# A perceiver block on one core: fp4 weight units loaded and dequantised in another rhythm, with zero products in the last context tiles

## The chip, the cores and the metric

One core of one Trainium2 chip runs the whole program. The metric is the device time in microseconds of one execution, as the median of several runs. The program drives five instruction streams: TensorE (PE) for matrix products and transposes, VectorE (DVE), ScalarE (ACT), GpSimd (POOL) and SyncE (SP), which here only issues DMA transfers. [...]

## What is computed

A latent array x of 64 rows and 256 columns passes three residual layers.

```python
x = x + cross_attention(layernorm(x), ctx)       # ctx: 6272 x 256, 32 heads of 8, q and k RMS-normalised
x = x + self_attention(layernorm(x))             # 16 heads of 128; wq, wk, wv, wo are fp4 codes times scales
x = x + expert_ffn(layernorm(x))                 # shared expert of 352, top 2 of 8 experts of 176
# the weights of the second layer:
w = codes * repeat(scales, 32, axis=0)           # one scale for 32 rows of a column
```

The codes and scales arrive as fp32. The product `codes * scales` has to be done on the chip for all four matrices, 256 x 2048 each for q, k and v, and 2048 x 256 for o.

## The kernel before

The cross attention streams the context in T = 49 tiles of 128 rows. For a tile, SP loads it transposed (`load`), DVE rounds it to `ctx_hi` (L544), POOL makes the rest `ctx_lo` (L348), and PE projects it to keys and values in six products of 512 columns (L796, L799, L802). ACT squares the keys (L419), DVE sums (L550), ACT makes the inverse root (L429, L433), DVE scales the keys (L568) and casts them to two fp16 parts (L575), POOL makes the third part (L354), and SP transposes the parts into `kT` by a DMA transpose (`turn`, L276). Then PE makes the scores with the 64 queries (L764, 32 products of 64 columns), ACT their exponentials in two halves (L407), and PE the weighted values, which gather in one PSUM bank over all tiles (L775).

The stages run against each other, staggered. In step c, PE does the scores of tile c, the values of tile c-1 and the projection of tile c+5; DVE and ACT normalise the keys of tile c+4, POOL makes `ctx_lo` of tile c+6 and the third key part of tile c+3. The scores of a tile wait until both exponentials of the tile before are done. PE, ACT and DVE run steps 2 to 41 in a hardware loop of eight steps a pass; steps before and behind are written out. POOL and SP are written out entirely. From step 44 there is no tile left to project.

The second layer's weights are cut into UNITS = 16 units of 128 x 1024 numbers: 12 of q, k and v (their scales are 128 x 512, used for both halves) and 4 of o (scales 128 x 1024). `w_all` keeps all of them; the scales pass through a ring of two buffers, `s_ring`. SP issues in step t of its own list `turn(t-7)` and `load(t)`, then at every third t the codes of a unit (one DMA of 512 KB, L279) and one t later its scales (L285, 256 KB read, or L288, 512 KB). POOL does `w = w * s` for a whole unit in one instruction (L340) behind the key part of every third step from step 3. Five small transfers (biases, the gate and its ids) go out at t = 2 to 6 (L313). Behind all of these SP issues the expert weights, five rounds of 704 KB and 352 KB (L293, L294).

Behind the loop DVE copies the gathered values (`o_sb`, L597), PE transposes them (L811), does 16 products of zeros (`keep_busy`, L725) while DVE makes x1 and its layer norm, transposes h (L718), waits for all units, and projects (L824). The output projection is L875, the experts L914 and L930.

```python
u, piece = divmod(t - LAG, DEQ)                  # SP: LAG = 7, DEQ = 3
if 0 <= u < UNITS and piece == 0: load_codes(u)
if 0 <= u < UNITS and piece == 1: load_scales(u)
```

Of the kernel before, what the change touches and what calls it, by code (L numbers as in the profile page):

```python
# [19 lines left out]
ALU = mybir.AluOpType  # L20
AX_X = mybir.AxisListType.X

P = 128
N = 64
D = 256
DC = D // P
# [19 lines left out]
RING = 2  # L46
# [3 lines left out]
UNITS = 4 * NSL  # L50
E, TOPK, H, HS = 8, 2, 176, 352
# [10 lines left out]
DEQ0, DEQ = 3, 3  # L62
# [51 lines left out]
def perceiver(nc, x, ctx_t, xwq, xwkv, codes, scales, wo_scales, qkv_bias, bo, gate_w, gate_bias,  # L114
              up_w, down_w, eye, expert_ids, out):
    with ExitStack() as stack:
# [26 lines left out]
        s_ring = sb("s_ring", [P, RING, WS])  # L143
# [90 lines left out]

        codes_in = [sem(f"codes_in{k}") for k in range(RING)]
        scales_in = [sem(f"scales_in{k}") for k in range(RING)]
        ring_free = [sem(f"ring_free{k}") for k in range(RING)]

# [20 lines left out]
        def _(sp):  # L259
# [18 lines left out]
            def load_codes(u):  # L278
                sp.dma_start(w_all[:, u], codes[:, u]).then_inc(codes_in[u % RING], 16)  # L279

            def load_scales(u):

                sp.wait_ge(ring_free[u % RING], u // RING + 1)
                if u < NQKV:
                    sp.dma_start(s_ring[:, u % RING, 0:512], scales[u].unsqueeze(0).to_broadcast(  # L285
                        [P // NB, NB, 512])).then_inc(scales_in[u % RING], 16)
                else:
                    sp.dma_start(s_ring[:, u % RING], wo_scales[u - NQKV].unsqueeze(0).to_broadcast(  # L288
                        [QB, P // QB, WS])).then_inc(scales_in[u % RING], 16)
# [11 lines left out]
            for t in range(2, T + LAG):  # L301
# [4 lines left out]
                u, piece = divmod(t - LAG, DEQ)  # L306
                if 0 <= u < UNITS and piece == 0:
                    load_codes(u)
                if 0 <= u < UNITS and piece == 1:
                    load_scales(u)  # L310
                if 2 <= t < 2 + len(small):
                    dst, src = small[t - 2]
                    sp.dma_start(dst, src).then_inc(ready("small_in"), 16)  # L313
# [7 lines left out]
        def _(pool):  # L321
# [4 lines left out]
            for k in range(RING):  # L326
                pool.memset(s_ring[0:1, k, 0:1], 0.0).then_inc(ring_free[k], 1)
# [3 lines left out]
            def dequantise(u):  # L331

                pool.wait_ge(codes_in[u % RING], (u // RING + 1) * 16)
                pool.wait_ge(scales_in[u % RING], (u // RING + 1) * 16)
                if u < NQKV:
                    w = w_all[:, u].rearrange("p (c n) -> p c n", c=DC)
# [5 lines left out]
            for c in range(FIRST, LAST + 1):  # L342
# [16 lines left out]
                if 0 <= u < UNITS and piece == 0:  # L359
                    dequantise(u)  # L360
# [653 lines left out]
```

## Time and profile before

| what | us |
|---|---|
| median of 3 runs | 228.83 |
| lowest and highest | 228.49 and 233.12 |
| the profiled execution | 229.14 |
| its span, first to last instruction | 227.3 |

In the span PE is busy 201.3 us, DVE 132.6, ACT 148.0 and POOL 107.4. The profile's times within the span count from its start. Matrix products are pipelined, so their recorded durations overlap; the distance of two starts says what one costs. An fp32 product is recorded as two. "PEclk" is the clock that PE was granted, as a share of 2.4 GHz (0.50 is 1.2 GHz); in a stretch with a change it is a mean. The words "<-issue" behind an idle time say that the engine waited for nothing that the profile shows.

### The profile page before, as it was taken

Reading aid. Unit: us, or ns where it says so; the run is one execution under the profiler, and the core shown is the slowest. Engines: PE = TensorE matmul, PEld = TensorE weight load, DVE = VectorE, ACT = ScalarE, POOL = GpSimd, SP = SyncE. Lnnn points to the kernel's source line nnn. Section 1 sums busy time; section 2 is a strip of 40 time slices with the busy share of each in tenths; the row PEclk is TensorE's granted clock in tenths of the full one; section 3 lists DMA queues with packets and bytes.
Section 4 is the critical chain, followed back from the end, with each engine's and each line's share of the span. In section 5 each row is a group of like instructions: output and inputs, shape, how many; then the busy total and the mean of one; then the engine's idle time right before and its main releaser. Section 6 shows DMA issues by size and latency. Waiting matters only on the chain.

```text
span 227.3 us, 9309 instructions
## 1 busy us (share of the span) xinstructions
PE 201.3 (89%) x3757; PEld 131.7 (58%) x3757; DVE 132.6 (58%) x324; ACT 148.0 (65%) x285; POOL 107.4 (47%) x125
## 2 busy tenths in 40 slices
PE   7786699799999999999999999898673899998994
PEld 2454477477777767676777777575452433554442
DVE  1668648367776776886867868757200422644721
ACT  3355688598989889889898898879852012413230
POOL 4334547746677586775785876847620000000000
PEclk9799999999999999999999999999758599999999
DMA  5418999999899799999998989899989860000000
GB/s 187 126 29 199 191 262 214 205 170 214 219 229 213 216 203 221 219 186 252 234 207 208 269 185 250 199 269 181 240 242 338 213 164 9 3 0 0 0 3 12
DMA packets 66674, 39.66 MB, mean 174 GB/s; under 512 B 53863, under 2 KB 60455, under 8 KB 66655
## 3 DMA queue, kind: packets, MB, share of 16 engines
q1 hardware_dynamic: 66223, 38.95, 78.2%
q10 hardware_dynamic: 432, 0.46, 0.6%
q8 instruction: 12, 0.20, 0.4%
q14 instruction: 7, 0.06, 0.1%
HBM read 26.48 MB, written 0.07 MB: 117 GB/s over the span
## 4 chain that ended last, share of the span: by engine, by line
PE 57%; issue 14%; ACT 9%; DVE 8%; DMA 7%; POOL 2%; SPq 1%; ACTq 0%; DVEq 0%
PE ps L775 12%; PE ps L796 8%; PE ps L764 6%; PE ps L802 6%; PE ps L799 6%; DMA kT<-k 5%; PE ps L824 5%; ACT room L407 4%; PE ps L914 3%; PE ps L930 2%; PE ps L725 2%; ACT k_sq L419 2%; ACT k_ln L429 2%; PE ps L875 2%; DVE k_n L568 2%
## 5 line engine op out<-in xcount | busy, mean ns | idle before, releaser
L407 ACT ACTIVATE room<-ps 128x1024 f32<-128x1024 f32 x98 | 100.2, 1027 | 15.8 <-PE ps L764 15.4
L348 POOL TENSOR_TENSOR ctx_lo<-ctx_f,ctx_hi 128x256 fp32r<-128x256 f32 x49 | 36.4, 743 | 53.3 <-DVE ctx_hi L544 51.2
L775 PE MATMUL ps<-room,v_flat 128*17 128x128 f32 x1568 | 55.9, 284 | 3.5 <-issue 3.5
L796 PE MATMUL ps<-wkv_hi,ctx_hi 128*128 128x512 f32 x98 | 43.4, 443 | 3.2 <-DVE k_n L568 1.7
L775 PEld LDWEIGHTS ps<-room,v_flat 128*17 128x17 f32 x1568 | 40.4, 100 | 7.5 <-issue 4.0
L575 DVE CAST k<-k_n 128x512 f16<-128x512 f32 x49 | 40.5, 826 | 2.6
L799 PE MATMUL ps<-wkv_lo,ctx_hi 128*128 128x512 f32 x98 | 39.0, 398 | 0.4 <-DVE wkv_lo L500 0.4
L340 POOL TENSOR_TENSOR w_all<-w_all,s_ring 128x1024 f32<-128x1024 f32 x16 | 38.0, 2380 | 0.0
L568 DVE TENSOR_TENSOR k_n<-ps,k_r 128x256 f32<-128x256 f32 x49 | 20.8, 425 | 25.5 <-ACT k_r L433 25.5
L354 POOL TENSOR_TENSOR k<-k_n,k 128x256 f16<-128x256 f32 x49 | 33.1, 675 | 3.5 <-DVE k L575 3.5
L764 PEld LDWEIGHTS ps<-qT,kT 24*128 24x128 f16 x1568 | 15.1, 94 | 28.0 <-ACT room L407 14.3
L802 PE MATMUL ps<-wkv_hi,ctx_lo 128*128 128x512 f32 x98 | 31.2, 400 | 0.0
L550 DVE TENSOR_REDUCE k_ss<-k_sq 128x32 f32<-128x256 f32 x49 | 20.4, 415 | 16.6 <-ACT k_sq L419 15.9
L764 PE MATMUL ps<-qT,kT 24*128 24x64 f16 x1568 | 21.2, 192 | 9.4 <-ACT room L407 3.5
L796 PEld LDWEIGHTS ps<-wkv_hi,ctx_hi 128*128 128x128 f32 x98 | 18.3, 187 | 16.1 <-issue 10.7
L429 ACT ACTIVATE k_ln<-k_ss,eps_rms 128x32 f32<-128x32 f32 x49 | 16.0, 327 | 9.5 <-DVE k_ss L550 9.5
L802 PEld LDWEIGHTS ps<-wkv_hi,ctx_lo 128*128 128x128 f32 x98 | 18.7, 191 | 4.4
L419 ACT ACTIVATE k_sq<-ps 128x256 f32<-128x256 f32 x49 | 18.5, 378 | 3.7 <-PE ps L802 3.7
L799 PEld LDWEIGHTS ps<-wkv_lo,ctx_hi 128*128 128x128 f32 x98 | 18.6, 190 | 2.9 <-DVE wkv_lo L500 0.8
L559 DVE COPY v_flat<-ps 128x256 f32<-128x256 f32 x45 | 18.6, 412 | 0.0
L544 DVE CAST ctx_hi<-ctx_f 128x256 fp32r<-128x256 f32 x48 | 13.6, 283 | 0.1
L365 ACT ACTIVATE rs<-mv,eps_ln 64x1 f32<-64x1 f32 x3 | 0.9, 294 | 19.3 <-DVE mv L475 19.3
(113 smaller groups left out, 137.0 us busy)
## 6 DMA issues: line engine op xcount, KB each, us to landing
w_all<-codes SPq DMA_DIRECT2D x16, 512.0 KB, 4.5
ctx_f<-ctx_t SPq DMA_DIRECT2D x48, 128.0 KB, 3.2
up_sb<-up_w SPq DMA_DIRECT2D x5, 704.0 KB, 9.7
s_ring<-scales SPq DMA_DIRECT2D x12, 256.0 KB, 3.8
s_ring<-wo_scales SPq DMA_DIRECT2D x4, 512.0 KB, 5.0
dn_sb<-down_w SPq DMA_DIRECT2D x5, 352.0 KB
kT<-k SPq DMA_TRANSPOSE x49, 4.0
wkv_f<-xwkv ACTq DMA_DIRECT2D x1, 256.0 KB, 3.1
```

Of the source, the lines that this page charges most:

```text
L340: nc.gpsimd.tensor_tensor(w, w, s, ALU.mult).then_inc(ring_free[u % RING], 1)
L348: nc.gpsimd.tensor_tensor(ctx_lo[:, split.slot(2)], ctx_f[:, split.slot(4)], ctx_hi[:, split.slot(2)].bitcast(F32), ALU.subtract).then_inc ...
L354: nc.gpsimd.tensor_tensor(key_part(keys, 2), k_n[:, keys.slot(2)].rearrange("p (h d) -> p h d", d=XD), key_part(keys, 0), ALU.subtract).th ...
L407: nc.scalar.activation(probs[:, t.slot(2), banks].rearrange("p g n -> p (g n)"), ps[:, banks, :].rearrange("p g n -> p (g n)"), ACT.Exp).t ...
L419: nc.scalar.activation(k_sq[:, a], ps_kv[a][:, 0:D], ACT.Square).then_inc(sq_done, 1)
L568: nc.vector.tensor_tensor(kn, ps_kv[r.slot(2)][:, 0:D].rearrange("p (h d) -> p h d", d=XD), k_r[:, r.slot(2)].unsqueeze(2).to_broadcast([P ...
L575: nc.vector.tensor_copy(key_parts(r)[:, :, 0:2, :], kn.unsqueeze(2).to_broadcast([P, XH, 2, XD])).then_inc(k1_done, 1)
L764: last = nc.tensor.matmul(ps[:, g, c * N:(c + 1) * N], kT[rows, t.slot(4), c], qT[rows, c], start=(c == 0), stop=(c == KC - 1), skip_group ...
L775: last = nc.tensor.matmul(ps_o[CT * j:CT * j + VW, g * P:(g + 1) * P], v_sb[:, t.slot(8), 2 * c + half], probs[:, t.slot(2), 2 * half:2 * ...
L796: nc.tensor.matmul(ps_kv[a], ctx_hi[:, a, c], wkv_hi[:, c], start=(c == 0), stop=False)
L799: nc.tensor.matmul(ps_kv[a], ctx_hi[:, a, c], wkv_lo[:, c], start=False, stop=False)
L802: last = nc.tensor.matmul(ps_kv[a], ctx_lo[:, a, c], wkv_hi[:, c], start=False, stop=(c == DC - 1))
```

## The change

The ring holds scales as RING = 4 slots of 128 x 512; a unit of o takes two neighbouring slots. Each unit has its own semaphore `unit_in[u]`, which three transfers raise, and one counter `unit_done` replaces the ring's.

SP issues the codes of a unit in two halves of 256 KB. Units 0 to 2 go out whole at t = 4, 5 and 6, before any transpose. Units 3 to 13 follow piece by piece, one piece a step in a rhythm of four: first half, second half, scales, and in the fourth step one of the small transfers while there are any. Units 14 and 15 go out behind the last transpose, ahead of the expert weights.

POOL multiplies a unit in three pieces (columns 0 to 171, 172 to 343 and 344 to 511 of both rows of 512), one a step: units 0 to 11 in steps 0 to 35, unit 12 in steps 39 to 41, unit 13 in 45 to 47, units 14 and 15 behind the last step.

PE does four products of zeros into bank 7 in every step from 44, and waits for 12 units before the projections and for all 16 before the output projection.

```diff
-RING = 2
+RING = 4
+EARLY, LATE = 3, 14
-DEQ0, DEQ = 3, 3
+DEQ_AT = [3 * u + 3 * max(0, u - NQKV + 1) for u in range(LATE)]
+THIRDS = ((0, 172), (172, 344), (344, 512))
...
-            def load_codes(u):
-                sp.dma_start(w_all[:, u], codes[:, u]).then_inc(codes_in[u % RING], 16)
+            def load_codes(u, half):
+                cols = slice(half * 512, (half + 1) * 512)
+                sp.dma_start(w_all[:, u, cols], codes[:, u, cols]).then_inc(unit_in[u], 16)
             def load_scales(u):
-                sp.wait_ge(ring_free[u % RING], u // RING + 1)
                 if u < NQKV:
...
+                    if u >= RING:
+                        sp.wait_ge(unit_done, u - RING + 1)
...
+                    k = DC * (u % 2)
+                    sp.wait_ge(unit_done, u - 1 if u >= LATE else NQKV - RING + k + DC)
...
+            def load_early(t):
+                u = t - (LAG - EARLY)
+                if u >= 0:
+                    for half in range(2):
+                        load_codes(u, half)
+                    load_scales(u)
+            def load_piece(t):
+                u, piece = divmod(t - LAG, 4)
+                u += EARLY
+                if EARLY <= u < LATE and piece < 2:
+                    load_codes(u, piece)
+                if EARLY <= u < LATE and piece == 2:
+                    load_scales(u)
+                if u < EARLY + len(small) and piece == 3:
+                    dst, src = small[u - EARLY]
+                    sp.dma_start(dst, src).then_inc(ready("small_in"), 16)
...
-            def dequantise(u):
-                pool.wait_ge(codes_in[u % RING], (u // RING + 1) * 16)
-                pool.wait_ge(scales_in[u % RING], (u // RING + 1) * 16)
+            def dequantise(u, piece):
+                if piece == 0:
+                    pool.wait_ge(unit_in[u], 3 * 16)
...
-                nc.gpsimd.tensor_tensor(w, w, s, ALU.mult).then_inc(ring_free[u % RING], 1)
+                lo, hi = THIRDS[piece]
+                done = nc.gpsimd.tensor_tensor(w[:, :, lo:hi], w[:, :, lo:hi], scale[:, :, lo:hi], ALU.mult)
+                if piece == len(THIRDS) - 1:
+                    done.then_inc(unit_done, 1)
...
+                if t.i is None and t.c >= T - PROJ:
+                    keep_busy(4, 7)
...
-            for k in range(RING):
-                pe.wait_ge(ring_free[k], UNITS // RING + 1)
+            pe.wait_ge(unit_done, NQKV)
...
             pe.wait_ge(pT_out, 2)
+            pe.wait_ge(unit_done, UNITS)
             join_heads(0)
```

SP's stream at its start, kernel before, from the transfer of tile 4 on (`kT<-k` is a key transpose, `s_ring` holds scales):

```order
L268 DMA ctx_f<-ctx_t 128x256
L313 DMA gate_sb<-gate_w 128x16
L268 DMA ctx_f<-ctx_t 128x256
L313 DMA gb_sb<-gate_bias 128x8
L268 DMA ctx_f<-ctx_t 128x256
L313 DMA iota<-expert_ids 128x8
L276 DMA_TRANSPOSE kT<-k 128x8x128
L268 DMA ctx_f<-ctx_t 128x256
L279 DMA w_all<-codes 128x1024
```

And the same place in the changed kernel, where the first row covers tiles 1 to 4:

```order
L269 DMA ctx_f<-ctx_t 128x256 x4
L281 DMA w_all<-codes 128x512 x2
L288 DMA s_ring<-scales 128x1x512
L269 DMA ctx_f<-ctx_t 128x256
L281 DMA w_all<-codes 128x512 x2
L288 DMA s_ring<-scales 128x1x512
L269 DMA ctx_f<-ctx_t 128x256
L281 DMA w_all<-codes 128x512 x2
L288 DMA s_ring<-scales 128x1x512
L277 DMA_TRANSPOSE kT<-k 128x8x128
L269 DMA ctx_f<-ctx_t 128x256
L281 DMA w_all<-codes 128x512
```

Nine transfers of weights moved ahead of the first transpose, and the small ones left that place.

POOL's stream in the loop, kernel before, over three steps (`ctx_lo`, the third key part, and a unit's product):

```order
L348 TENSOR_TENSOR ctx_lo<-ctx_f,ctx_hi 128x256
L354 TENSOR_TENSOR k<-k_n,k 128x32x8
L340 TENSOR_TENSOR w_all<-w_all,s_ring 128x1024
L348 TENSOR_TENSOR ctx_lo<-ctx_f,ctx_hi 128x256
L354 TENSOR_TENSOR k<-k_n,k 128x32x8
L348 TENSOR_TENSOR ctx_lo<-ctx_f,ctx_hi 128x256
L354 TENSOR_TENSOR k<-k_n,k 128x32x8
```

The changed kernel, over three steps:

```order
L375 TENSOR_TENSOR ctx_lo<-ctx_f,ctx_hi 128x256
L381 TENSOR_TENSOR k<-k_n,k 128x32x8
L365 TENSOR_TENSOR w_all<-w_all,s_ring 128x2x172
L375 TENSOR_TENSOR ctx_lo<-ctx_f,ctx_hi 128x256
L381 TENSOR_TENSOR k<-k_n,k 128x32x8
L365 TENSOR_TENSOR w_all<-w_all,s_ring 128x2x172
L375 TENSOR_TENSOR ctx_lo<-ctx_f,ctx_hi 128x256
L381 TENSOR_TENSOR k<-k_n,k 128x32x8
L365 TENSOR_TENSOR w_all<-w_all,s_ring 128x2x168
```

One product of 1024 columns every third step became a piece in each of the three.

PE's stream behind the loop, kernel before, from the scores of step 46 on (`qT,kT` scores, `room,v_flat` values, `zeros` products of zeros):

```order
L764 MATMUL ps<-qT,kT 128x64 x32
L775 MATMUL ps<-room,v_flat 17x128 x16
L764 MATMUL ps<-qT,kT 128x64 x32
L775 MATMUL ps<-room,v_flat 17x128 x16
L764 MATMUL ps<-qT,kT 128x64 x32
L775 MATMUL ps<-room,v_flat 17x128 x32
L811 MATMUL ps<-ident,o_sb 64x128 x8
L725 MATMUL ps<-zeros 128x512 x16
```

The changed kernel, from the scores of step 47 on:

```order
L794 MATMUL ps<-qT,kT 128x64 x32
L805 MATMUL ps<-room,v_flat 17x128 x16
L755 MATMUL ps<-zeros 128x512 x4
L794 MATMUL ps<-qT,kT 128x64 x32
L805 MATMUL ps<-room,v_flat 17x128 x16
L755 MATMUL ps<-zeros 128x512 x4
L805 MATMUL ps<-room,v_flat 17x128 x16
L755 MATMUL ps<-zeros 128x512 x8
L843 MATMUL ps<-ident,o_sb 64x128 x8
L755 MATMUL ps<-zeros 128x512 x16
```

Each step has four more products behind its values, and steps 49 and 50 put eight between the last values and the transposes of `o_sb`.

## Rows read from the trace of the kernel before

**Rows 1.** Busy time by stretch: start:end, length, engines, PEclk, DMA share, GB/s.
```profile
8.00:16.00 8.00, 6.95 (x22) 4.13 (x22) 4.42 (x12) 4.18 (x14) 2.78 (x4) 0.79 0.23 51
42.30:142.00 99.70, 98.39 (x2348) 71.08 (x2351) 72.48 (x164) 88.27 (x166) 70.44 (x77) 1.00 1.01 219
162.60:172.80 10.20, 8.55 (x219) 5.99 (x210) 0.00 (x0) 5.82 (x6) 3.84 (x2) 0.54 1.14 275
```

**Rows 2.** Timeline of PE: starts of scores of tiles 6, 7, 8, 40, 41.
```profile
42.26 0.21 PE L764 MATMUL ps<-qT,kT 24*128 24x64 f16 x5 [1.69 <-issue]
45.11 0.27 PE L764 MATMUL ps<-qT,kT 24*128 24x64 f16 x12
48.04 0.35 PE L764 MATMUL ps<-qT,kT 24*128 24x64 f16 x22
143.99 0.21 PE L764 MATMUL ps<-qT,kT 24*128 24x64 f16 x4
148.16 0.22 PE L764 MATMUL ps<-qT,kT 24*128 24x64 f16 x5 [1.17 <-DMA kT<-k]
```

**Rows 3.** Timeline, GpSimd and VectorE, two neighbouring tiles of the loop.
```profile
96.76 0.43 DVE L575 CAST k<-k_n 128x512 f16<-128x512 f32 x1
97.11 0.28 DVE L544 CAST ctx_hi<-ctx_f 128x256 fp32r<-128x256 f32 x1
98.80 2.38 POOL L340 TENSOR_TENSOR w_all<-w_all,s_ring 128x1024 f32<-128x1024 f32 x1
99.61 1.86 DVE L575 CAST k<-k_n 128x512 f16<-128x512 f32 x1
101.39 0.28 DVE L544 CAST ctx_hi<-ctx_f 128x256 fp32r<-128x256 f32 x1
```

**Rows 4.** The page's groups (busy us, mean ns) and DMA issues (us to landing).
```profile
L407 ACT ACTIVATE room<-ps 128x1024 f32<-128x1024 f32 x98 | 100.2, 1027 | 15.8 <-PE ps L764 15.4
L348 POOL TENSOR_TENSOR ctx_lo<-ctx_f,ctx_hi 128x256 fp32r<-128x256 f32 x49 | 36.4, 743 | 53.3 <-DVE ctx_hi L544 51.2
...
kT<-k SPq DMA_TRANSPOSE x49, 4.0
```

**Rows 5.** Timeline of PE from tile 45's scores: start, duration, line, idle time before.
```profile
159.83 0.41 PE L764 MATMUL ps<-qT,kT 24*128 24x64 f16 x32 [1.44 <-ACT room L407]
160.17 1.07 PE L775 MATMUL ps<-room,v_flat 128*17 128x128 f32 x32
162.44 0.61 PE L764 MATMUL ps<-qT,kT 24*128 24x64 f16 x32 [1.20 <-ACT room L407]
...
166.78 0.24 PE L764 MATMUL ps<-qT,kT 24*128 24x64 f16 x3 [1.02 <-issue]
...
169.69 3.05 PE L775 MATMUL ps<-room,v_flat 128*17 128x128 f32 x59
176.23 0.62 PE L775 MATMUL ps<-room,v_flat 128*17 128x128 f32 x5 [3.49 <-issue]
177.65 1.91 PE L811 MATMUL ps<-ident,o_sb 128*64 128x128 f32 x8 [0.79 <-DVE o_sb L597]
179.35 5.07 PE L725 MATMUL ps<-zeros 128*128 128x512 f16 x16
184.35 0.33 PE L718 MATMUL ps<-ident,h_sb 64*128 64x64 f32 x2
```

**Rows 6.** DMA queues, 173.5 to 176.3 us: packets, MB, share of 16 engines.
```profile
q8 instruction: 1, 0.02, 2.9%
```

**Rows 7.** SP's issues of the first transpose and expert weights; the chain at 22.
```profile
16.05 1.35 SPq L276 DMA_TRANSPOSE kT<-k  x1
...
22.18 5.89 DMA kT<-k
...
163.27 0.58 SPq L293 DMA_DIRECT2D up_sb<-up_w  x1
```

**Rows 8.** Timeline of PE, zero products behind the output projection, full clock.
```profile
206.41 2.98 PE L725 MATMUL ps<-zeros 128*128 128x512 f16 x13
```

More of the change, by code:

```diff
@@ L233, in perceiver @@
         scores_mm, exp_done, pv_done = sem("scores_mm"), sem("exp_done"), sem("pv_done")
-        codes_in = [sem(f"codes_in{k}") for k in range(RING)]
-        scales_in = [sem(f"scales_in{k}") for k in range(RING)]
-        ring_free = [sem(f"ring_free{k}") for k in range(RING)]
+        unit_in = [sem(f"unit_in{u}") for u in range(UNITS)]
+        unit_done = sem("unit_done")
         qk_mm, v_mm, q_out, k_out, v_out = sem("qk_mm"), sem("v_mm"), sem("q_out"), sem("k_out"), sem("v_out")
@@ L305, in _ @@
                     load(t)
[L306 to L313, printed above, removed]
+                if t < LAG:
+                    load_early(t)
+                else:
+                    load_piece(t)
+            for u in range(LATE, UNITS):
+                for half in range(2):
+                    load_codes(u, half)
+                load_scales(u)
             for r in range(NR):
@@ L357, in _ @@
                         key_part(keys, 0), ALU.subtract).then_inc(k2_done, 1)
-                u, piece = divmod(c - DEQ0, DEQ)
-                if 0 <= u < UNITS and piece == 0:
-                    dequantise(u)
+                for u, first in enumerate(DEQ_AT):
+                    if first <= c < first + len(THIRDS):
+                        dequantise(u, c - first)
+            for u in range(LATE, UNITS):
+                for piece in range(len(THIRDS)):
+                    dequantise(u, piece)
         def layernorm_act(act, name):
@@ L720, in transpose_h, with keep_busy @@
                 last.then_inc(ready(name + "_hT_mm"), 1)
-            def keep_busy(n):
+            def keep_busy(n, bank=3):
                 for _ in range(n):
-                    nc.tensor.matmul(ps[:, 3, :], zeros[:, 0:P], zeros[:], start=True, stop=True, skip_group_check=True)
+                    nc.tensor.matmul(ps[:, bank, :], zeros[:, 0:P], zeros[:], start=True, stop=True, skip_group_check=True)
             def contract(dst, rhs, **flags):
@@ L816, in _ @@
             pe.wait_ge(ready("ln2_hT"), 1)
-            for k in range(RING):
-                pe.wait_ge(ring_free[k], UNITS // RING + 1)
+            pe.wait_ge(unit_done, NQKV)
             def project(dst, w, s):
```

18 lines of the change are left out of this document (9 added, 9 removed).

## The prediction

> **What bounds the kernel now.** I read the stretches first. Through the loop over the context tiles TensorE (PE) is busy 98.39 of 99.70 us at the full clock (granted 1.00), while GpSimd has 70.44 and VectorE 72.48 [rows 1]: there the bound is PE, and only what makes PE late can be won. The starts of each tile's score products say how much that is. An undisturbed tile takes 48.04 - 45.11 = 2.93 us, say 2.94. From tile 7 (45.11) to tile 40 (143.99) are 33 tiles in 98.88 us, 33 x 2.94 = 97.0, so 1.86 us are lost in small pieces. Two single losses stand beside them: 1.69 us in the middle of tile 6's scores, released by nothing ("issue"), and 1.17 us before tile 41, where the transposed keys had not landed [rows 2].
>
> Where do the small pieces come from? The timeline of one tile with a dequantisation: the GpSimd product runs 2.38 us from 98.80, and VectorE's cast that starts at 99.61 takes 1.86 us, ending just behind it; the next cast for ctx_hi starts at 101.39 [rows 3]. The same cast takes 0.43 us in the tile before, which has no product (96.76). So a GpSimd product holds this VectorE cast until it ends. By the Trainium skill ("SBUF — State Buffer", section "Who interferes with whom") the two share a port pair that one holds exclusively for a whole instruction. By that rule, with which the 1.86 us agrees, a third would still hold the cast, only for less.
>
> Last the end of the loop, in the timeline. From tile 45 PE has no projection, and the clock falls: granted 0.54 in 162.60 to 172.80 [rows 1]. Tiles 45 to 46 take 162.44 - 159.83 = 2.61 us, set by ScalarE's two exponentials. PE then stands still twice with "issue", 3.49 us before 176.23 and 1.02 before 166.78. Between the two stops run the 3 scores left of tile 47, a tile's 32 values, a tile's 32 scores and the 59 values in the row of 169.69, 126 matmuls with their weight loads, 252 instructions plus a few waits [rows 5]. Inside the second stop, 173.5 to 176.3, the queue table has one packet of the queue "instruction", 0.02 MB [rows 6]. I read both stops, and that of tile 6, as PE waiting for the next block of its program, some 256 instructions, which is asked for when the previous block is entered (166.78) and comes behind the weights that SP issues from 163.27 on [rows 7]: 176.23 - 166.78 = 9.45 us.
>
> The Trainium skill ("Runtime: NRT & Kernel Launch", section "Instruction fetch mechanics") speaks against this reading: it calls the cost of entering a new 16 KiB block mostly hidden. By it the after kernel would have no such stop; that is the third case below. The trace does not agree, its 3.49 us decide.
>
> **The change, part by part.** The profiled execution took 229.14 us (span 227.3, 1.8 around it); the median of the runs is 228.83, 0.3 less. I sum against 229.14 and take 0.3 off at the end.
>
> Head. Nine loads of 256 KB (2.36 MB) now stand ahead of the first key transpose (issued at 16.05). From 8 to 16 us the DMA engines are at 0.23, 51 GB/s [rows 1], so the room is there, but only from where SP releases tile 4's load. In those 8 us, 0.77 x 8 = 6.2 us are free; at 275 GB/s (the rate of 162.60 to 172.80) 1.7 MB pass, leaving 0.66 MB or 2.4 us in front of the first transpose [rows 7]; if they run faster, nothing. In exchange the third transpose, on which tile 2 waits, 5.89 us in the chain (22.18 to 28.07), finds pieces of 256 KB instead of 512; at the median of all transposes, 4.0 [rows 4], it lands 1.9 us earlier. If the first is late by d, the tiles behind it follow at PE's pace and tile 2 is late by d less about 1.5 (now 28.07 and a signal; at PE's pace 16.05 + 4.7 for the landing + 2 x 2.94 = 26.6). I take d = 1.9: +0.3 us, bounds -1.6 and +2.
>
> Loop, GpSimd. Product time for 1024 columns is 2.38 us, for 256 columns 0.74 [rows 3, 4]; a third (344 columns) is about 0.74 + 88/768 x 1.64 = 0.93. Bounds 0.79 (a third of 2.38) and 1.6 (twice, if the two separate rows of 172 cost). Ring of dependences in a tile: ctx_hi cast to product start 98.80 - 97.11 = 1.69, product end (101.18) to the next ctx_hi cast 0.21, together 1.90 + third = 2.83 us. That is under 2.94, so PE stays the bound, although now 36 tiles in a row carry a piece. I take back 1.6 of the 1.86 us (bounds 0 and 1.86). The counts agree: 14 x 3 thirds instead of 16 products.
>
> Loop, DMA. A unit now comes every four tiles instead of three, so 192 KB a tile instead of 256. At tile 41 only transposes and small pieces are in the queue: -1.1 us (bounds 0 and -1.17). The code stop of tile 6: its block waits behind 256 KB rather than 512 KB, about 1 us less at 219 GB/s: -1.0 (bounds 0 and -1.69). The last loop units have little slack (unit 11 is loaded about two tiles ahead of its product); a late one holds GpSimd alone, whose transposes have a tile to spare. Loop together: -3.7.
>
> Tail, from tile 45 (159.83) to the transposes of h (184.35), 24.5 us. Zero products start 0.215 us apart at the full clock (13 in 2.98 us, less the last one's run) [rows 8], so four a tile are 0.86 us; at half the clock twice that. At full clock scores 0.41, values 1.07 and 0.86 make 2.34 us, inside the 2.61, so they are hidden behind ScalarE and PE is busy nine tenths of the time; I expect the clock to hold. Scores of tile 48 start at 3 x 2.61 = +7.8. The stop of 1.02 goes: at tile 45 only transposes are in flight now. The second block limit moves: 8 instructions for each zero group put it into the first quarter of tile 48's values, needed at +9.7 (scores 0.41, one exponential of 1.03 [rows 4], signals and seven matmuls). It is asked for at +5.5, two us into the loads of units 14 and 15, behind some 1.3 MB (4.7 us at 275 GB/s) and a transpose; with landing and restart I take +12.0, a stop of 2.3 us (bounds +9.7, +15). Then 25 value matmuls 0.8, the eight last zero products 1.7 (the copy of o_sb, 176.85 to 177.65 in the trace, lies beside them, so 0.9 of it is new), eight transposes 1.1 at full clock instead of 1.91, and the chain on VectorE from there to h, 184.35 - 179.56 = 4.8 in the trace, of which 0.9 is PE still at its 16 zero products that started at 179.35 with a slow clock; 3.9 remain. +12.0 + 0.8 + 1.7 + 1.1 + 3.9 = +19.5 against +24.5: -5.0. A drop of the clock after the stop would give back up to 3; I take -3.5 (bounds -6.7 and +0.8). The late units are dequantised by GpSimd until about 176, beside VectorE's short chain: up to 0.9, inside these bounds. PE asks for them only before the output projection, some 18 us further on.
>
> Sum: +0.3 - 3.7 - 3.5 = -6.9. 229.14 - 6.9 - 0.3 = 221.9 us.
>
> **The rivals.** (a) The code block comes as late as before, 9.45 us after it is asked for: +15. PE is cold by then, 25 values 1.5, eight zero products 3.4, transposes 1.5 (between 1.1 and 1.91), chain 3.9: +25.3 against +24.5. 228.84 + 0.3 - 3.7 + 0.8 = 226.2. For it: the backlog is larger than before, 7.3 MB instead of 5.3 behind the loop. Against: it has just begun when the block is asked for. (b) The block is there in time. The last values end at +10.9, zero products +12.6, transposes +13.7, h at +17.7: -6.8. 228.84 - 3.4 - 6.8 = 218.6. For it: the change's loads are in smaller pieces. Against: three stops in this trace. (c) The other side: the third costs more than 1.03 us, so that the ring 1.90 + third passes 2.94 and sets the pace of 36 tiles. At 1.4 us the ring is 3.3, 36 x 0.37 = +13.3, and the 1.6 is not won: 228.84 + 0.3 - 2.1 - 3.5 + 13.3 = 236.8. For it: the piece now holds VectorE in every tile and its access is in two rows; against: the row for 256 columns, 0.74. (d) The change does nothing: the head gives back what the loop saves and the last zero products eat the warm clock: 228.5.
>
> **How the numbers follow.** Forecast 0.50, (a) 0.25, (b) 0.12, (c) 0.06, (d) 0.07. The range reaches from 217.0 (case b with a better head) to 228.0 (most of a), leaving (c), part of (d) and the edges outside. About 2% (224.3 us) is what a measurement of this kernel tells from no change. Faster than that: 0.92 of the forecast, a fifth of (a), all of (b), together 0.63. Slower: (c), 0.06. Within: 0.31.
>
> **What would show it.** Thirds of 0.8 to 1.0 us, the cast (L575 before) no longer at 1.8 us, 33 tiles in at most 97.3 us; no DMA wait at tile 41; tile 2's scores between 26.6 and 30; granted clock 1.00 from tile 45 to 48 with starts 2.61 apart; one "issue" stop in tile 48's values of 1 to 4 us; transposes of o_sb 13 to 16 us behind tile 45's scores. Wrong would make it: thirds above 1.03 us with tiles of more than 3 us; a clock near 0.5 with zero products 0.43 us apart; the first scores three us late; the stop in tile 48 above 5 us.

## The result and the profile after

The changed kernel takes 220.21 us in the median (219.25 to 220.91, 4 runs), the kernel before beside it 228.66 us (225.54 to 233.12). The ratio is 0.967, interval 0.957 to 0.978: faster, and 1.7 us below the forecast of 221.9. The profiled execution took 220.11 us, its span is 218.3. Medians here are over all runs; the ratios and their intervals leave out executions more than 1.5% above their kernel's fastest, and the profiles of e2, e4, e8 and e13 below are of such long executions.

The difference of the two spans, 9.0 us, is read off the starts of four pieces of work on TensorE (times within the span):

| what starts | before | after | gained in between |
|---|---|---|---|
| scores of tile 10 | 53.91 | 53.99 | -0.08 |
| scores of tile 45 | 159.83 | 156.74 | 3.17 |
| transposes of h | 184.35 | 175.33 | 5.93 |
| end of the span | 227.3 | 218.3 | 0 |

The stretches of the changed kernel, columns as in [rows 1], with the tail from the scores of tile 45 on as the third:

```profile
8.00:16.00 8.00, 6.97 (x22) 3.89 (x22) 4.28 (x12) 3.86 (x14) 2.59 (x5) 0.79 0.77 222
42.30:142.00 99.70, 99.48 (x2348) 71.88 (x2340) 61.56 (x170) 89.70 (x169) 72.75 (x98) 1.00 0.96 203
156.70:170.00 13.30, 12.42 (x312) 7.31 (x313) 1.54 (x3) 8.09 (x10) 6.10 (x8) 1.00 0.81 240
```

PE is now busy 99.48 of 99.70 us in the loop, VectorE 61.56 instead of 72.48 although it does the same work, GpSimd 2.3 us more than before. In the head the DMA engines went from 0.23 to 0.77. In the tail the granted clock is 1.00, where before it was 0.54 in [rows 1].

GpSimd and VectorE in two neighbouring tiles, against [rows 3]:

```profile
97.98 0.92 POOL L365 TENSOR_TENSOR w_all<-w_all,s_ring 128x344 f32<-128x344 f32 x1
...
98.87 0.43 DVE L605 CAST k<-k_n 128x512 f16<-128x512 f32 x1
99.21 0.29 DVE L574 CAST ctx_hi<-ctx_f 128x256 fp32r<-128x256 f32 x1
...
100.92 0.92 POOL L365 TENSOR_TENSOR w_all<-w_all,s_ring 128x344 f32<-128x344 f32 x1
...
101.81 0.43 DVE L605 CAST k<-k_n 128x512 f16<-128x512 f32 x1
102.28 0.29 DVE L574 CAST ctx_hi<-ctx_f 128x256 fp32r<-128x256 f32 x1
```

Each tile carries a piece of 0.92 us, and the cast starts where the piece ends and takes its undisturbed 0.43 us. The page's groups, against [rows 4], say it for the whole run:

```profile
L365 POOL TENSOR_TENSOR w_all<-w_all,s_ring 128x344 f32<-128x344 f32 (+1 forms) x48 | 43.5, 911 | 5.8 <-DMA s_ring<-wo_scales 5.8
L605 DVE CAST k<-k_n 128x512 f16<-128x512 f32 x49 | 22.1, 451 | 2.5
...
kT<-k SPq DMA_TRANSPOSE x49, 3.4
```

PE's first tiles and two in the loop, against [rows 2]:

```profile
27.85 0.41 PE L794 MATMUL ps<-qT,kT 24*128 24x64 f16 x32
...
30.23 0.61 PE L805 MATMUL ps<-room,v_flat 128*17 128x128 f32 x11 [1.21 <-issue]
...
36.22 1.06 PE L805 MATMUL ps<-room,v_flat 128*17 128x128 f32 x30 [0.17 <-issue]
...
51.97 0.49 PE L805 MATMUL ps<-room,v_flat 128*17 128x128 f32 x9 [0.22 <-issue]
...
53.99 0.41 PE L794 MATMUL ps<-qT,kT 24*128 24x64 f16 x32
...
145.07 0.41 PE L794 MATMUL ps<-qT,kT 24*128 24x64 f16 x32
...
148.01 0.41 PE L794 MATMUL ps<-qT,kT 24*128 24x64 f16 x32
```

The stop with "issue" in tile 6 is gone; three others, 1.60 us together, stand in tiles 2, 4 and 9 (what more kernels say of these stops is below, under "Head and first tiles"). Tile 41 starts with no wait for its keys. The tail, against [rows 5]:

```profile
156.74 0.41 PE L794 MATMUL ps<-qT,kT 24*128 24x64 f16 x32 [0.47 <-ACT room L437]
...
158.09 1.04 PE L755 MATMUL ps<-zeros 128*128 128x512 f16 x4
159.32 0.41 PE L794 MATMUL ps<-qT,kT 24*128 24x64 f16 x32 [0.19 <-ACT room L437]
...
161.89 0.49 PE L794 MATMUL ps<-qT,kT 24*128 24x64 f16 x32 [0.19 <-ACT room L437]
...
164.53 0.41 PE L794 MATMUL ps<-qT,kT 24*128 24x64 f16 x32 [0.17 <-ACT room L437]
...
166.84 0.41 PE L805 MATMUL ps<-room,v_flat 128*17 128x128 f32 x7
167.52 0.94 PE L805 MATMUL ps<-room,v_flat 128*17 128x128 f32 x25 [0.28 <-issue]
168.39 1.90 PE L755 MATMUL ps<-zeros 128*128 128x512 f16 x8
170.13 1.04 PE L843 MATMUL ps<-ident,o_sb 128*64 128x128 f32 x8
171.00 3.62 PE L755 MATMUL ps<-zeros 128*128 128x512 f16 x16
175.33 0.33 PE L748 MATMUL ps<-ident,h_sb 64*128 64x64 f32 x2 [0.71 <-DVE h_sb L518]
```

The tiles start some 2.6 us apart, as before; the 3.49 us stop has become one of 0.28, behind 7 of tile 48's last 32 values. SP's issues show what is in the queue by then:

```profile
160.28 1.04 SPq L281 DMA_DIRECT2D w_all<-codes  x2
161.36 0.56 SPq L293 DMA_DIRECT2D s_ring<-wo_scales  x1
...
163.66 0.60 SPq L319 DMA_DIRECT2D up_sb<-up_w  x1
```

### The profile page after: what moved, and what is told of

It is laid out like the page before. It is cut to its first block, busy times and chain, and to the rows that moved or that the text cites. A ratio compares the mean times of both kernels' runs of the same rounds, so it can differ in the third digit from the quotient of the medians.

```text
span 218.3 us, 9395 instructions
## 1 busy us (share of the span) xinstructions
PE 202.4 (93%) x3785; PEld 130.9 (60%) x3785; DVE 115.6 (53%) x324; ACT 147.2 (67%) x285; POOL 111.6 (51%) x155
## 4 chain that ended last, share of the span: by engine, by line
PE 81%; DMA 5%; ACT 4%; DVE 4%; issue 3%; POOL 1%; ACTq 0%; DVEq 0%
PE ps L805 22%; PE ps L828 13%; PE ps L834 10%; PE ps L831 10%; PE ps L794 8%; PE ps L855 5%; PE ps L946 3%; DMA kT<-k 3%; DMA ctx_f<-ctx_t 2%; ACT room L437 2%; PE ps L962 2%; PE ps L906 2%; PE ps L755 1%; PE ps L864 1%; PE ps L894 1%
## 5 line engine op out<-in xcount | busy, mean ns | idle before, releaser
L375 POOL TENSOR_TENSOR ctx_lo<-ctx_f,ctx_hi 128x256 fp32r<-128x256 f32 x49 | 36.2, 738 | 46.9 <-DVE ctx_hi L574 44.3
L805 PE MATMUL ps<-room,v_flat 128*17 128x128 f32 x1568 | 53.7, 274 | 1.9 <-issue 1.9
L365 POOL TENSOR_TENSOR w_all<-w_all,s_ring 128x344 f32<-128x344 f32 (+1 forms) x48 | 43.5, 911 | 5.8 <-DMA s_ring<-wo_scales 5.8
L828 PE MATMUL ps<-wkv_hi,ctx_hi 128*128 128x512 f32 x98 | 44.1, 450 | 1.8 <-ACT v_flat L452 1.1
L805 PEld LDWEIGHTS ps<-room,v_flat 128*17 128x17 f32 x1568 | 38.8, 97 | 5.9 <-issue 3.4
L794 PEld LDWEIGHTS ps<-qT,kT 24*128 24x128 f16 x1568 | 14.6, 93 | 21.3 <-ACT room L437 13.6
L605 DVE CAST k<-k_n 128x512 f16<-128x512 f32 x49 | 22.1, 451 | 2.5
L794 PE MATMUL ps<-qT,kT 24*128 24x64 f16 x1568 | 20.3, 189 | 2.8 <-ACT room L437 1.9
L755 PE MATMUL ps<-zeros 128*128 128x512 f16 x66 | 17.7, 415 | 0.0
```

Of the source, the lines that this page charges most:

```text
L365: done = nc.gpsimd.tensor_tensor(w[:, :, lo:hi], w[:, :, lo:hi], scale[:, :, lo:hi], ALU.mult)
L375: nc.gpsimd.tensor_tensor(ctx_lo[:, split.slot(2)], ctx_f[:, split.slot(4)], ctx_hi[:, split.slot(2)].bitcast(F32), ALU.subtract).then_inc ...
L605: nc.vector.tensor_copy(key_parts(r)[:, :, 0:2, :], kn.unsqueeze(2).to_broadcast([P, XH, 2, XD])).then_inc(k1_done, 1)
L794: last = nc.tensor.matmul(ps[:, g, c * N:(c + 1) * N], kT[rows, t.slot(4), c], qT[rows, c], start=(c == 0), stop=(c == KC - 1), skip_group ...
L805: last = nc.tensor.matmul(ps_o[CT * j:CT * j + VW, g * P:(g + 1) * P], v_sb[:, t.slot(8), 2 * c + half], probs[:, t.slot(2), 2 * half:2 * ...
L828: nc.tensor.matmul(ps_kv[a], ctx_hi[:, a, c], wkv_hi[:, c], start=(c == 0), stop=False)
```

## The experiments

The ratios are to the runs of the kernel before beside each kernel, with their 95% intervals; every number but the medians and ratios comes from the kernel's own profiled execution. "Tail" is from the scores of tile 45 to the transposes of h; "stop" is PE idle with "issue" from tile 45 to 48.

| kernel | median | ratio | tile 10 | tiles 10 to 44 | tail | stop |
|---|---|---|---|---|---|---|
| before | 228.66 | 1 | 53.91 | 103.07 | 24.52 | 1.02 + 3.49 |
| after | 220.21 | 0.967 (0.957-0.978) | 53.99 | 99.90 | 18.59 | 0.28 |
| e1, before with zero products | 227.71 | 0.992 (0.987-0.998) | 53.94 | 103.55 | 22.91 | 2.21 |
| e2, after without them | 221.13 | 0.960 (0.947-0.973) | 55.58 | 99.91 | 21.06 | 2.41 |
| e3, after with whole products | 222.29 | 0.976 (0.965-0.987) | 53.46 | 102.53 | 18.38 | none |
| e4, before, experts held | 222.47 | 0.974 (0.964-0.985) | 55.78 | 102.79 | 20.40 | 1.18 |
| e5, after, experts held | 220.55 | 0.963 (0.956-0.970) | 52.99 | 99.90 | 18.40 | none |
| e7, after, no zeros in the last two steps | 218.60 | 0.955 (0.947-0.962) | 53.40 | 99.90 | 17.49 | none |
| e8, e5 without zeros | 223.60 | 0.975 (0.966-0.983) | 54.67 | 99.90 | 22.11 | 2.99 |
| e9, after, one early unit, four late | 220.82 | 0.966 (0.959-0.973) | 51.73 | 99.90 | 18.99 | none |
| e10, no zeros, all late loads held | 219.71 | 0.967 (0.949-0.984) | 53.11 | 99.91 | 17.67 | none |
| e11, e7 with all late loads held | 217.86 | 0.959 (0.947-0.971) | 53.23 | 99.90 | 17.02 | none |
| e12, e9 with e7's diff, late products held | 218.67 | 0.964 (0.950-0.978) | 51.38 | 99.91 | 17.60 | none |
| e13, e12 with all late loads held | 226.77 | 0.978 (0.967-0.989) | 54.16 | 99.90 | 17.87 | 0.67 |

### The parts of the change, one at a time

Zero products alone, added to the kernel before (`keep_busy` there gets the bank as a second argument):

```diff
+                if t.i is None and t.c >= T - PROJ:
+                    keep_busy(4, 7)
```

> The kernel before plus four zero products in each step from 44, nothing else. Theory (code blocks): the zero products keep the clock at 1.00 but also move the block limit forward into the first quarter of tile 48's values, while the queue is as full as before, so the block still comes 9 to 9.5 us after PE asks for it: a stop of 5 to 6.5 us in tile 48, and 226 to 230 us, within 2% of before. Rival (clock alone is what the tail gained): granted 1.00 to the end and 5 to 6 us less, 223 us.

Measured: 227.71 us (224.96 to 233.30), ratio 0.992 (0.987 to 0.998). The tail is 1.6 us shorter.

```profile
171.38 0.41 PE L775 MATMUL ps<-room,v_flat 128*17 128x128 f32 x7
174.00 1.61 PE L775 MATMUL ps<-room,v_flat 128*17 128x128 f32 x25 [2.21 <-issue]
```

The stop moved from behind 27 values of the last 32 to behind 7 of them. That is what 40 more instructions in front of it (20 zero products, each a weight load and a matmul) do if it belongs to a fixed place in PE's program, and I read this as shown: in the changed kernel and in e2 it stands at 7 and 27 again. The zero products alone are worth 1.2 us in the medians, of the change's 8.5. The time fell into the expected range, but the price of the stop was wrong: 5 to 6.5 us expected, 2.21 measured, because PE went on 7.4 us after it had entered the block before, 126 matmuls earlier (166.63 to 174.00), and not 9 to 9.5. The rival, 223 us from the clock alone, is out, although the clock was granted 1.00 up to 174. In this kernel two tiles of the end, 44 and 47, also wait 1.02 and 1.12 us for their keys, among the units that are still being loaded.

The change without the zero products:

```diff
-                if t.i is None and t.c >= T - PROJ:
-                    keep_busy(4, 7)
```

> The changed kernel without its zero products in the steps from 44. Theory: the clock falls to 1.2 GHz again behind tile 45 (zero products of the 16 group 0.43 us apart, value groups 1.91 instead of 1.07), but the code block, asked for while little is queued, comes in time, so only 2 to 3 us are lost: 222 to 223.5. Rival (the zero products carry the whole gain of the tail): 226 us, 5.9 more than the changed kernel.

Measured: 221.13 us (217.73 to 224.22), ratio 0.960. The profiled execution, of 224.22 us, has the stop at 2.41 us and the clock granted 0.66 in 165 to 170 us; its tail is 2.5 us longer than the changed kernel's. So the theory's block in time did not come about in it. Between the medians only 0.9 us are left, less than the scatter of these 4 runs, and by the ratios (0.960 and 0.967) this kernel is not behind the changed one at all. These runs don't show that the zero products, all seven groups together, save time inside the change; later kernels look at their two effects one by one (e5 against e8, e10 against e11).

The change with each unit multiplied in one instruction, in every third step (units 12 and 13 in steps 39 and 45):

```diff
-THIRDS = ((0, 172), (172, 344), (344, 512))
+THIRDS = ((0, 512),)
```

> The changed kernel with each unit's product as one instruction of 2.38 us in the first of its three steps; loads and zero products as changed. Theory (the product holds VectorE's cast, which makes PE late): the cast takes 1.8 us again in these steps and the tiles 10 to 44, 99.9 us in the changed kernel, take 101.5 to 102.5; the time is 221.5 to 223. Rival (the slower rhythm of the loads is what the loop gained): tiles stay 2.94 us apart and the time within 0.5 us of the changed kernel.

Measured: 222.29 us (221.34 to 224.38), ratio 0.976 (0.965 to 0.987). Tiles 10 to 44 take 102.53 us instead of 99.90. One tile with a product, on GpSimd and VectorE:

```profile
98.10 2.38 POOL L365 TENSOR_TENSOR w_all<-w_all,s_ring 128x1024 f32<-128x1024 f32 x1
...
98.92 1.85 DVE L605 CAST k<-k_n 128x512 f16<-128x512 f32 x1
100.69 0.28 DVE L574 CAST ctx_hi<-ctx_f 128x256 fp32r<-128x256 f32 x1
```

The held cast of [rows 3] is back, and with it 2.6 us; the thirds are worth 2.1 us in the medians. From tile 15 on the distances of the starts read 2.94, 2.94, 3.04, 2.94, 2.94, 3.19, 2.94, 2.94, 3.13 us and so on: nearly every tile with a product costs 0.1 to 0.4 us more, in this kernel and in the one before, and none does in the changed one. One distance of e3, from tile 35 to 36, is 3.94 us, which nothing in before answers to. There GpSimd's product had waited 0.85 us for its scales, started at 126.17, and held VectorE's other cast, that of `ctx_hi`, for 2.34 us (126.57) instead of 0.28; PE then waited 0.83 us for `k_n`. From tile 10 on, late keys cost 0.22 us in all here (before tile 39) instead of 1.17: that part of the gain is the spacing of the loads.

### What the stop behind the loop waits for

The kernel before, its experts' loads issued only when `o_sb` is copied (all other instructions as before):

```diff
+            sp.wait_ge(ready("o_sb"), 1)
             for r in range(NR):
```

> The kernel before with the expert weights issued only when o_sb is copied, instead of behind the last key transpose. Theory (PE waits for its own code behind queued weights): the stop of 3.49 us in tile 48 and most of the 1.02 us before go, the clock behind them recovers earlier, and the time is 4 to 5 us less, 224. Rival (the stop has nothing to do with the DMA queue): both stops stay and the time is the same or more, since the weights come later.

Measured: 222.47 us (222.27 to 226.65), ratio 0.974 (0.964 to 0.985). One line in the kernel before gives 6 us in the medians, 3.4 to 8.3 by the interval of the ratio. The profiled execution took 226.65 us; its tile 10 starts 1.9 us late, and its tail is 4.1 us shorter than before:

```profile
168.20 0.20 PE L765 MATMUL ps<-qT,kT 24*128 24x64 f16 x3 [1.18 <-issue]
...
171.08 3.61 PE L776 MATMUL ps<-room,v_flat 128*17 128x128 f32 x64
175.51 1.92 PE L812 MATMUL ps<-ident,o_sb 128*64 128x128 f32 x8 [0.82 <-DVE o_sb L598]
```

The 3.49 us stop is gone, all 64 values run through; the first stop, ahead of which units are still being loaded, stays. So the second stop of the kernel before is caused by the weights in flight. It isn't an entry into a new block as such: the block is entered at the same instruction in both kernels.

The same hold in the changed kernel, with and without the zero products (the diff of e4, and for the second that of e2):

> The changed kernel with the expert weights issued only when o_sb is copied. Theory (the block of code comes in time because little is queued when it is asked for): the last stop of 0.28 us in tile 48 goes and nothing else changes, 219.9 us, since the weights are needed some 30 us later. Rival (the loads behind the loop still cost the tail something through the shared queue): 2 us less than the changed kernel.

> The changed kernel without zero products in the steps from 44 and with the expert weights issued only when o_sb is copied: the price of the clock alone, beside the run that only holds the weights. Theory (zero products do two things, they keep the clock and they make PE ask for its code before the queue is full): no stop in tile 48 here, clock 1.2 GHz for two stretches, 1.5 to 2.5 us more than the run that only holds the weights. Rival (all of their gain is the clock): 5 us more.

Measured: 220.55 us (219.03 to 221.1) and 223.60 us (221.88 to 226.01). With zeros there is no stop, and the median is that of the changed kernel: its stop of 0.28 us had nothing to give. Without zeros I expected no stop either, and that was wrong:

```profile
167.63 0.61 PE L806 MATMUL ps<-room,v_flat 128*17 128x128 f32 x11 [0.28 <-ACT room L438]
...
171.23 0.62 PE L806 MATMUL ps<-room,v_flat 128*17 128x128 f32 x5 [2.99 <-issue]
```

This profiled execution took 226.01 us; the ratios, 0.963 and 0.975, also put the kernel without zeros behind, by 2.7 us. Units 14 and 15 alone, 2 MB, were in flight. The next pair holds them too, again without and with zero products:

```diff
+            sp.wait_ge(ready("o_sb"), 1)
             for u in range(LATE, UNITS):
```

and for e10 the diff of e2, for e11 that of e7 (below).

> The changed kernel without zero products in the steps from 44, and with units 14 and 15 and the expert weights issued only when o_sb is copied, so that nothing but transposes is queued when PE asks for its code. Theory (the stop that stayed with only the experts held, 2.99 us, came from the late units in the queue): no stop above 0.5 us in tile 48; what is left to the clock is the transposes of o_sb at 1.9 us instead of 1.0 and the 16 zero products behind them. 220 to 221.5. Rival (without zero products PE always stops there): the stop of 2.5 to 3 us stays, 223.5.

> As the run before, but with zero products in steps 44 to 48. Beside it the difference is the clock alone: theory 1.5 to 2.5 us less, 218 to 218.8, with granted 1.00 to the end; the late products of GpSimd now fall behind the layer norm, so its chain from the transposes of o_sb to those of h takes 5.0 us or less (5.5 with the products beside it). Rival (waiting with the loads is paid at the output projection, which needs units 14 and 15): 1 to 3 us more, an idle PE before the output projection.

Measured: 219.71 us (218.54 to 222.32) and 217.86 us (216.94 to 219.06), ratios 0.967 and 0.959. Neither has a stop, so e8's came from units 14 and 15. With the stop out of the way the two differ by the clock alone. The stretch 160 to 165 us, columns as in [rows 1], first e10:

```profile
160.00:165.00 5.00, 3.69 (x112) 2.70 (x116) 0.00 (x0) 3.38 (x4) 0.47 (x1) 0.55 0.03 6
```

and e11:

```profile
160.00:165.00 5.00, 4.63 (x136) 2.80 (x135) 0.00 (x0) 3.67 (x5) 0.58 (x1) 1.00 0.06 13
```

Without zero products PE had waited 1.44, 1.16 and 1.16 us in front of three tiles from 155.88 on and was then granted 0.55, that is nearly all at 1.2 GHz; with them it stayed at 2.4 GHz. The tails are 17.67 and 17.02 us, the medians 1.85 apart (4 runs each, whose ranges overlap by 0.5 us; without one execution of e10 at 222.32 us the medians are 218.70 and 217.86). So the zero products do two separate things. They hold the clock: 0.65 us of tail, and the medians don't settle whether it is more. And with the late units in flight the stop is gone (e8 against e5, about 3 us); in e1, with the expert weights in flight from 163.69 on, a stop of 2.21 us stays in spite of them.

### The last eight zero products

```diff
-                if t.i is None and t.c >= T - PROJ:
+                if t.i is None and T - PROJ <= t.c < T:
```

> The changed kernel with zero products only in steps 44 to 48, so without the eight between the last values and the transposes of o_sb. Theory (they lie on the chain): the transposes start 0.8 us after the last value instead of 1.75, 0.9 us less, 219.3. Rival (they hold the clock over the copy of o_sb): the clock falls behind them and the time is 1 us more or higher.

Measured: 218.60 us (218.09 to 221.81), ratio 0.955, 1.6 us below the changed kernel. The transposes of `o_sb` start 0.81 us behind the last value, bound by VectorE's copy. In the changed kernel that copy was done at 168.50 + 0.69 = 169.19, while PE was at its eight zero products until 170.13: 0.94 us in the way, the 0.9 of the prediction. The tails differ by 1.10 us; what the medians differ by beyond that is inside the scatter of the runs.

### The head, and four units behind the loop

One early unit instead of three, eleven in the loop, one every four steps and still in thirds, four behind it:

```diff
-EARLY, LATE = 3, 14
+EARLY, LATE = 1, 12
-DEQ_AT = [3 * u + 3 * max(0, u - NQKV + 1) for u in range(LATE)]
+DEQ_AT = [0] + [4 * u - 1 for u in range(1, LATE)]
```

> The changed kernel with one unit in the head instead of three and four behind the loop instead of two (all four of wo), dequantised from step 4u-1. Theory (what the loop does not win in its first ten tiles is the queue that the head's 2.4 MB and the first pieces leave behind, in which the first key transpose and PE's code blocks wait): the first transpose lands within 4.7 us, tile 10 starts 1 to 2.5 us earlier than 53.99, and the time is 218 to 219.5. Rival (the first ten tiles lose the same with any load): tile 10 within 0.5 us, and 1 to 2 us more behind the loop because the four late units hold VectorE there, 221.5.

Measured: 220.82 us (220.43 to 221.83), no gain, where 218 to 219.5 was expected. Tile 10 starts 2.3 us earlier, tile 48 at 162.33, and then it is lost. VectorE's chain behind the loop:

```profile
169.37 1.09 DVE L638 TENSOR_TENSOR x<-x_sb,o_cat 64x256 f32<-64x256 f32 x1
...
172.51 0.94 DVE L518 TENSOR_SCALAR h_sb<-x,mv,rs 64x256 f32<-64x256 f32 x1
173.31 1.08 DVE L643 TENSOR_TENSOR q_f<-x,bo_sb 64x256 f32<-64x256 f32 x1
```

The same add and norm in e11, where GpSimd stands still until 173.96 (and alike in the kernel before):

```profile
169.96 0.42 DVE L639 TENSOR_TENSOR x<-x_sb,o_cat 64x256 f32<-64x256 f32 x1
...
172.44 0.51 DVE L519 TENSOR_SCALAR h_sb<-x,mv,rs 64x256 f32<-64x256 f32 x1
```

The add takes 0.42 us and the norm 0.51 there; in e9 the late units' products run beside them. PE then waits 1.63 and 0.79 us, its clock falls (0.68 granted in 175 to 180), and its first 16 projections take 5.35 us instead of 3.65. To mend that, e12 lets GpSimd wait for `hT` before the last two units, and leaves out the last eight zero products:

```diff
+                if u == UNITS - 2:
+                    pool.wait_ge(ready("ln2_hT"), 1)
```

> One unit in the head, four behind the loop, zero products in steps 44 to 48, and GpSimd's last two units multiplied only when h is transposed. Theory (the 2.3 us that one early unit gained in the head were given back by GpSimd's products holding VectorE in the layer norm, and by the clock that fell for it): the head's gain stays, h's transposes at 171.5 to 172.5 us, projections at full clock, 216 to 217.5. Rival (the gain goes back into the queue behind the loop: code or expert weights late): 219 or more.

Measured: 218.67 us (216.59 to 220.08), ratio 0.964 (0.950 to 0.978); the projections run at 3.65 us again. The median is above the expected 216 to 217.5, the profiled execution, 216.59 us, is not. Last, e12 with the late loads and the experts held until `o_sb` (the diff of e11):

> The kernel with one early unit, twelve in the loop and no zero products in the last two steps, and besides the loads of the four late units and of the experts held back until o_sb is copied. Theory (what is left of the gain sits in front of o_sb, and everything behind has room): the start stays as early as with one early unit (tile 10 at about 51.4), tile 48 at 161.5 to 162, no stop of PE in its values, transposes of o_sb at 165.9 to 166.4, h at 171.2 to 171.7; the four late units land behind 181, are ready before the output projection, and the experts' products find their weights: median 216 to 217.5. Rival (the held loads come too late): 4 MB of late units and 5 MB of expert weights issued from 166 on need some 35 us; the output projection waits for unit 15 or the expert products for their weights, 1 to 4 us, and the median is 218 to 221.

Measured: 226.77 us (221.7 to 230.44), ratio 0.978 (0.967 to 0.989). The rival (the held loads come too late) was right, and its price, 218 to 221 us, too low for the median. SP's issues, and PE's longest wait:

```profile
169.75 0.82 SPq L281 DMA_DIRECT2D w_all<-codes  x2
...
178.76 0.55 SPq L293 DMA_DIRECT2D s_ring<-wo_scales  x1
...
182.35 0.61 SPq L319 DMA_DIRECT2D up_sb<-up_w  x1
```

```profile
PE ps L949 <- DMA up_sb<-up_w: 6.0, 1, 6.0
```

SP waits 9.5 us for `o_sb`. Then four held units need the two places of the ring twice, so SP waits for GpSimd's products between them, 5.2 us in two waits. The experts behind are issued at 182.35, against 171.37 in e12 and 163.66 in the changed kernel. The expert products wait 6.0 us and start with a lower clock (0.74 granted in 200 to 210): from the transposes of h to the end 51.3 us instead of 43.0. The 0.67 us of the table stand in tile 47's scores, at the limit where the kernel before lost 1.02, with nothing but key transposes in the queue: a short stop doesn't need weights in flight. This execution took 227.94 us; against e12 the medians are 8.1 us apart, the ratios (0.978 and 0.964) only some 3. Another 2.8 us over e12 in the profile lie in the head, where both kernels are the same. PE's query projection, first in e12, then in e13:

```profile
9.32 1.08 PE L762 MATMUL ps<-wq_sb,hT 128*64 128x256 f32 x4
```

```profile
10.44 1.97 PE L763 MATMUL ps<-wq_sb,hT 128*64 128x256 f32 x4
```

The same four products take 1.08 us in one execution and 1.97 in the other, so PE ran at 2.4 GHz in one and 1.2 in the other, and the first key transpose is issued at 14.52 and 17.14 us. In e13 the slow products reach from 7.50 to about 13.7 us. Over all fourteen profiles this issue lies between 14.52 and 17.28: up to 15.52 in the five whose query projection took 1.61 us or less, from 16.02 on in the nine with 1.78 or more. The start of tile 10 therefore compares two heads only against this issue: behind it 37.9, 38.6 and 39.4 us in the three kernels with the old order of loads, 36.9 to 37.6 in seven of the eight with the new (39.6 in e2), and 36.2, 36.9 and 37.0 with one early unit. Of the 2.3 and 2.6 us that e9 and e12 seemed to win up to tile 10 against the changed kernel, 0.8 and 1.8 lie ahead of that issue and go with the clock of the one execution; about 0.6 us, the distance of the medians 37.4 and 36.9, may be the change's.

The fastest median is that of e11, 217.86 us, 1.1% below the changed kernel's; their runs, 216.94 to 219.06 and 219.25 to 220.91, don't overlap, but by the ratios to the kernel before beside each, 0.959 and 0.967, the intervals do.

## Why the prediction was right

The forecast of 221.9 us was 1.7 too high. The mechanisms held: the thirds free VectorE's cast, the spacing of the loads frees the keys, and the clock and the stop behind the loop make the tail. Up to tile 10 the sum was 0.8 us too hopeful, in the loop 0.5 and in the tail 2.4 too cautious; 0.4 lie between the profiled executions and the medians. That the first of these offset part of the last is luck.

**Head and first tiles.** Predicted +0.3 for the loads, -1.0 for tile 6's stop. Measured in the one profile: 0.08 us lost up to tile 10. The first transpose is late by less than reckoned: tile 0's scores start 5.71 us behind its issue instead of 4.67, 1.0 us and not 1.9, and tile 2's start at 27.85 instead of 28.19. The median landing is 3.4 us instead of 4.0. In this pair the term that failed is the stop: "its block waits behind 256 KB rather than 512 KB, about 1 us less". It is 1.69 us in one place before and 1.60 in three now. Over all profiles the term looks better: the stop in tile 6 took 1.69, 2.02 and 1.88 us in the three kernels with the old order of loads and is in none of the eight with the new, and the stops of the first ten tiles add up to 1.7, 2.6 and 2.8 us there and to 0.5 to 2.2, median 1.35, here. Whether the smaller loads did that, as the prediction has it, no kernel tests alone. Measured from the first transpose's issue, the new head and the first ten tiles together are about 1.2 us shorter (medians 38.6 and 37.4), of which the pair of profiles shows 0.2; the scatter is as large as the difference.

**Loop.** Predicted for the thirds -1.6, for the keys of tile 41 -1.1, together -2.7; measured -3.17. The third was priced at 0.93 us and took 0.91. With it tiles 10 to 44 take 99.90 or 99.91 us in all ten kernels that have thirds, 34 x 2.94, whatever stands before or behind, and 102.5 to 103.6 in the four that don't. What is left, 3.17 - 1.17 = 2.0, is the thirds', all of the 1.86 us that the prediction found and not only the 1.6 it took. By the Trainium skill ("SBUF — State Buffer", section "Who interferes with whom") a GpSimd product holds some VectorE instructions for its whole length; the trace agrees for the cast under a product of 2.38 us [rows 3]. The cast is not held by thirds, since they end as it starts (98.87), where the prediction had taken the rule to mean that a third still holds it, only for less.

**Tail.** Computed -5.0, taken -3.5, measured -5.93. By its steps, from tile 45's scores: tile 48 at +7.8 predicted, +7.79 measured; the limit behind 7 values of tile 48, as predicted; the restart at +12.0 predicted, +10.78 measured; transposes of `o_sb` +14.5, measured +13.39; h +19.5, measured +18.59. The terms that were off are the size of the stop, 2.3 us predicted and 0.28 measured, and the 1.5 us put aside for a clock drop behind it, which then didn't come: the granted clock is 1.00 up to 217 us. A third error worked the other way. The block was said to be needed at +9.7, from tile 48's scores and one exponential. But between the two PE does tile 47's values and four zero products, so tile 48's values start only at +10.10 (166.84) and the block is needed at +10.5. Case (b), the block in time, carried the same error: it has h at +17.7, and e5, which has no stop, at +18.40. (By its own terms its last values end at +10.5 and not +10.9, and the 0.37 us a tile of case (c) should be 0.36; neither changes the forecast.) That the block comes "behind some 1.3 MB and a transpose" is too simple: with all of this in the queue the packet of the queue "instruction" starts 3.0 us after the previous block is entered (162.09, the +5.5 of the prediction measured as +5.35), when 0.8 MB have moved. The result lies between the case of the block being there in time (218.6) and the forecast.

**The mechanism of the stop** stands, its size doesn't follow from the queue. That it belongs to a place in PE's program is shown by the count: in all five kernels that stop in tile 48 it stands before the same matmul of PE's stream, and that of tile 47 in before, e4 and e13 always 126 matmuls ahead of it. That weights in flight cause it is shown by e4 (3.49 to none) and e10 against e8 (2.99 to none). The Trainium skill ("Runtime: NRT & Kernel Launch", section "Instruction fetch mechanics") calls the cost mostly hidden. At this limit, in tile 48, that holds for nine kernels that don't stop and nearly for the changed one (0.28), and not for the other four, with 2.21 to 3.49 us; in the first tiles no kernel is free of stops. From the start of the packet to PE's next matmul all five kernels that stop take 2.4 to 2.7 us. How long the packet takes to start varies: in e4, whose queue is empty, 3.2 us after the entry into the previous block, in e5 2.5, in e8 6.0 with the same two units in flight as in e5, in the kernel before 6.8. The queues of e8 in half a microsecond around it (packets, MB, share of 16 engines):

```profile
q1 hardware_dynamic: 36, 0.13, 62.2%
q8 instruction: 1, 0.02, 12.2%
```

One packet among 36 of the loads. Why e8's packet starts 3.5 us later than e5's isn't settled. It is not that the block is asked for at another point of the loads' course: PE enters the previous block 2.1 us behind the issue of the first late load in e5 (159.21 and 161.32) and 2.0 us behind it in e8 (160.81 and 162.81). The two kernels differ in the zero products, and by what path these could matter no kernel tells.

**The others.** Rival (c), a third above 1.03 us, fell with 0.91. Rival (a), the block as late as before, was ruled out by the 0.28 us: PE went on 5.4 us behind the entry and not 9.45. Rival (d), no gain, was ruled out in all its parts but one: the last zero products do cost 0.9 us.

## What to carry to other kernels

Where GpSimd and VectorE share a tile's time, cut the GpSimd work to what fits into the gap of VectorE's chain and give every tile a piece; GpSimd's time in the loop went up by 2.3 us and 2 us came off the whole. Don't let bulk loads for a later stage start while the engine that bounds this one still has unrolled code to enter: one wait ahead of them was worth 6 us here, and the same wait ahead of loads that are needed soon cost 3 to 8. Zero products belong only in slots where the engine is idle anyway, and not in front of something that is ready (0.9 us here); their gain in the idle slots was small without loads in flight (0.65 us of tail) and about 3 us with them.

## What was not expected of the hardware

- The same head took 2.6 us more in one execution (e13) than in another (e12), because PE ran at 1.2 GHz instead of 2.4 from about 7.5 to 13.7 us (the query projection 1.97 or 1.08 us), behind the same zero products. So two profiles alone don't tell what a change in the head is worth.
- Stops for program blocks also stand in the first tiles, where only context tiles, transposes and units are in flight, 0.2 to 2.0 us each.
- A GpSimd product stretched VectorE's two-operand add (0.42 to 1.09 us) and its norm (0.51 to 0.94) with operands in SBUF, and not its copy from PSUM: that of `o_sb` takes 0.69 us in the changed kernel, where GpSimd's row of thirds runs from 167.16, and 0.69 in e11, where GpSimd stands still.
